# A decoder's first expert layer on one core: the down product of each expert as three rounded passes

## The chip, the cores and the metric

One core of one Trainium2 chip. The time is device microseconds (us) of one execution of the kernel, the median of several runs. A profiled execution comes with it; its records give the start and length of each instruction on the five engines: TensorE (PE, with its weight loads as PEld), VectorE (DVE), ScalarE (ACT), GpSimd (POOL) and SyncE (SP), which here only issues DMA transfers.

## What is computed

Two decoder layers over 4 sequences of 256 tokens with 256 features, each of self-attention, a second mixing block and a mixture of experts, with layer norms between. The change lies in the first layer's mixture of experts. There are 32 experts, each token goes to 4 of them, and each expert has room for 256 tokens. Cut to that part:

```python
buf = jnp.zeros((E, C, x.shape[1]), x.dtype).at[sorted_eid, pos].set(x[tok], mode='drop')
gu = jnp.einsum('ech,ehf->ecf', buf, w13)
g, u = jnp.split(gu, 2, axis=-1)
act = jax.nn.silu(g) * u
eo = jnp.einsum('eci,eih->ech', act, w2)
```

with E = 32, C = 256, h = 256 and i = 128. All of it is float32.

## The kernel before

The kernel is one program of stages, each with its own buffers and semaphores; within a stage each engine runs its own list of instructions in order, and they wait for each other on semaphores. The stage of the change is `layer0_experts`. The stage before it scatters the tokens' rows into `k.slots` in DRAM, 256 slots an expert, and the stage after it gathers the results from `k.out_slots`.

The experts go one after the other. Four make a round (`RING` = 4), and the rounds are a hardware loop with the first and the last (for VectorE the first two) written out. Weights and rows lie in rings of four buffers, most intermediate tiles in rings of two. For expert e:

- SP (`load`, `load_down`, `store`, L928 to L945) loads the rows (256 KB), w13 (256 KB) and w2 (128 KB), and stores the result (256 KB). In its round it issues, per expert e: rows and w13 of e + 4, w2 of e + 3, and the store of e - 2. The load of w2 waits until the down product of e - 1 is done, the store until the result of e - 2 has been copied out. Before the rounds it issues rows and w13 of experts 0 to 3, and then w2 of experts 0 to 2.
- TensorE: `turn` (L995) transposes the rows in four 128x128 pieces into PSUM. `up` multiplies with w13 in rounded passes, through the helper `product` (L76 to L78). `down` (L1015) multiplies the activations with w2 in two plain float32 matmuls, which the profile records as four. The order in the round is turn(e + 1), up(e), down(e - 1).
- ScalarE: `keep_rows` (L1037) copies the turned rows from PSUM as rounded values, `cut_high` (L1042) rounds w13 of e + 2, and L1056 takes the silu of the gate half. In that order.
- GpSimd: `cut_low` (L974) subtracts the rounded w13 from w13.
- VectorE: `rows_low` (L1069) subtracts the rounded rows from the turned ones, L1080 multiplies silu and up half into `actT`, `keep_out` (L1064) copies the down product to SBUF. In that order, for e + 1, e and e - 1.

A rounded product splits each operand x into a rounded part x.h (type fp32r) and a rest x.l = x - x.h, and adds three passes:

```python
pe.matmul(out, left[0], right[1], start=start, stop=False)
pe.matmul(out, left[0], right[0], start=False, stop=False)
return pe.matmul(out, left[1], right[0], start=False, stop=stop)
```

`Parts` holds the pair of tiles. ScalarE also issues one transfer of the next layer's weights (1 MB, `layer1_prefetch`) after its first round.

Of the kernel before, what the change touches and what calls it, by code (L numbers as in the profile page):

```python
# [8 lines left out]
P = 128  # L9
# [887 lines left out]
def layer0_experts(nc, k, I):  # L897

    RING = 4
    with ExitStack() as stack:  # L900
# [5 lines left out]
        rowsT = Parts(m, "e_rowsT", [P, 2, DC * CAP])  # L906
        silu = m.sb("e_silu", [P, 2, CAP])
        actT = m.sb("e_actT", [P, 2, CAP])
        out = m.sb("e_out", [P, RING, 2, D])
        turn_ps = m.ps("e_turn_ps", [P, 2, 512])  # L910
        up_ps = m.ps("e_up_ps", [P, 2, 512])
# [2 lines left out]
        w_in = [m.sem(f"e_w_in{r}") for r in range(RING)]  # L914
        w2_in = [m.sem(f"e_w2_in{r}") for r in range(RING)]
        w_high, w_low = m.sem("e_w_high"), m.sem("e_w_low")
        stored = k.stored
        turned = m.sem("e_turned")
        rowsT_high, rowsT_low = m.sem("e_rowsT_high"), m.sem("e_rowsT_low")
# [6 lines left out]
        with nc.Block() as block:  # L926
            @block.sync
            def _(sp):  # L928
                def load(e, r):
                    at_least(sp, turned, e - RING + 1)  # L930
                    sp.dma_start(rows[:, r], k.slots[bass.ds(e * CAP, CAP), :].rearrange("(s p) d -> p s d", p=P)
                                 ).then_inc(rows_in[r], 16)
                    at_least(sp, w_low, e - RING + 1)
                    sp.dma_start(w13[:, r], I["L0_ffn_w13"][bass.ds(e, 1)].rearrange("a (c p) f -> p (a c) f", p=P)
                                 ).then_inc(w_in[r], 16)

                def load_down(e, r):
                    at_least(sp, down_done, e - RING + 1)
                    sp.dma_start(w2[:, r], I["L0_ffn_w2"][bass.ds(e, 1)].rearrange("a p d -> p (a d)")
                                 ).then_inc(w2_in[r], 16)  # L940

                def store(e, r):
                    sp.wait_ge(out_kept, e + 1)
                    sp.dma_start(k.out_slots[bass.ds(e * CAP, CAP), :].rearrange("(s p) d -> p s d", p=P), out[:, r]
                                 ).then_inc(stored[r], 16)  # L945

                def emit(rnd, first, last):
                    for r in range(RING):
                        e = RING * rnd + r
                        if not last:  # L950
                            load(e + RING, r)
                        if not last or r == 0:
                            load_down(e + RING - 1, (r - 1) % RING)
                        if not first or r >= 2:
                            store(e - 2, (r - 2) % RING)
                sp.wait_ge(k.scattered, NT * TOP0 * 16)
                for e in range(RING):
                    load(e, e)
                for e in range(RING - 1):
                    load_down(e, e)  # L960
                emit(0, True, False)
                with sp.Fori(1, E0 // RING - 1) as rnd:
                    emit(rnd, False, False)
                emit(E0 // RING - 1, False, True)
                for r in range(RING - 2, RING):
                    store(E0 - RING + r, r)
                for r in range(RING):
                    sp.wait_ge(stored[r], 16 * (E0 // RING))

            @block.gpsimd  # L970
            def _(pool):
                def cut_low(e, r):
                    pool.wait_ge(w_high, e + 1)
                    pool.tensor_tensor(w13_p.l[:, r], w13[:, r], w13_p.h[:, r], ALU.subtract).then_inc(w_low, 1)  # L974
                with pool.Fori(0, E0 // RING) as rnd:
                    for r in range(RING):
                        cut_low(RING * rnd + r, r)
# [10 lines left out]
            @block.tensor  # L988
            def _(pe):
                def turn(e, r, rnd):  # L990
                    pe.wait_ge(rows_in[r], 16 * (rnd + 1))
                    at_least(pe, rowsT_low, e - 1)
                    for c in range(DC):
                        for s in range(2):
                            last = pe.transpose(turn_ps[:, r % 2, c * CAP + s * P:c * CAP + (s + 1) * P],  # L995
                                                rows[:, r, s, c * P:(c + 1) * P], k.ident[:, :])
                    last.then_inc(turned, 1)

                def up(e, r, rnd):
                    pe.wait_ge(w_low, e + 1)  # L1000
                    pe.wait_ge(rowsT_low, e + 1)
                    at_least(pe, act_done, e - 1)
                    for j in range(2):
                        for c in range(DC):
                            last = product(pe, up_ps[:, r % 2, j * CAP:(j + 1) * CAP],
                                           w13_p[:, r, c, j * I0:(j + 1) * I0],
                                           rowsT[:, r % 2, c * CAP:(c + 1) * CAP], c == 0, c == DC - 1)
                    last.then_inc(up_done, 1)

                def down(e, r, rnd):  # L1010
                    pe.wait_ge(w2_in[r], 16 * (rnd + 1))
                    pe.wait_ge(act_done, e + 1)
                    at_least(pe, out_kept, e - 1)
                    for s in range(2):
                        last = pe.matmul(down_ps[:, r % 2, s * D:(s + 1) * D], actT[:, r % 2, s * P:(s + 1) * P],  # L1015
                                         w2[:, r, :], start=True, stop=True)
                    last.then_inc(down_done, 1)

                turn(0, 0, 0)

                def emit(rnd, first, last):
                    for r in range(RING):
                        e = RING * rnd + r
                        if not (last and r == RING - 1):
                            turn(e + 1, (r + 1) % RING, rnd + (r == RING - 1))
                        up(e, r, rnd)
                        if not (first and r == 0):
                            down(e - 1, (r - 1) % RING, rnd - (r == 0))
                rounds(pe, emit)
                down(E0 - 1, RING - 1, E0 // RING - 1)  # L1030

            @block.scalar
            def _(act):
# [5 lines left out]
                def cut_high(e, r, rnd):  # L1039
                    act.wait_ge(w_in[r], 16 * (rnd + 1))  # L1040
                    at_least(act, up_done, e - RING + 1)
                    act.activation(w13_p.h[:, r], w13[:, r], ACT.Copy).then_inc(w_high, 1)  # L1042
                cut_high(0, 0, 0)
                keep_rows(0, 0)
                cut_high(1, 1, 0)

                def emit(rnd, first, last):
                    for r in range(RING):
                        e = RING * rnd + r
                        if not (last and r == RING - 1):  # L1050
                            keep_rows(e + 1, (r + 1) % RING)
                        if not (last and r >= RING - 2):
                            cut_high(e + 2, (r + 2) % RING, rnd + (r >= RING - 2))
                        act.wait_ge(up_done, e + 1)
                        at_least(act, act_done, e - 1)
                        act.activation(silu[:, r % 2, :], up_ps[:, r % 2, 0:CAP], ACT.Silu).then_inc(silu_done, 1)  # L1056
                rounds(act, emit, beside=layer1_prefetch)

            @block.vector
            def _(dve):  # L1060
# [6 lines left out]
                def rows_low(e, r):  # L1067
                    dve.wait_ge(rowsT_high, e + 1)
                    dve.tensor_tensor(rowsT.l[:, r % 2, :], turn_ps[:, r % 2, :], rowsT.h[:, r % 2, :], ALU.subtract  # L1069
                                      ).then_inc(rowsT_low, 1)  # L1070
                rows_low(0, 0)

                def emit(rnd, first, last):
                    for r in range(RING):
                        e = RING * rnd + r
                        if not (last and r == RING - 1):
                            rows_low(e + 1, (r + 1) % RING)
                        dve.wait_ge(silu_done, e + 1)
                        at_least(dve, down_done, e - 1)
                        dve.tensor_tensor(actT[:, r % 2, :], silu[:, r % 2, :], up_ps[:, r % 2, CAP:2 * CAP], ALU.mult  # L1080
                                          ).then_inc(act_done, 1)
                        if not (first and r == 0):
                            keep_out(e - 1, (r - 1) % RING, rnd - (r == 0))
                rounds(dve, emit, peeled=2)
                keep_out(E0 - 1, RING - 1, E0 // RING - 1)

# [1982 lines left out]
```

## Time and profile before

| | us |
|---|---|
| median of 3 runs | 1152.67 (1152.44 to 1154.89) |
| the profiled execution | 1150.72 |
| its span | 1148.8 |
| TensorE busy in the span | 1027.6 (89%) |
| VectorE, ScalarE, GpSimd busy | 722.9, 570.5, 473.5 |
| mean granted TensorE clock | 0.951 of full |

The experts' stage lies between about 392 and 489 us of the span. The span is what the trace covers; the profiled execution's own time is 1.9 longer, for what lies around it. Busy shares are means over stages that have different limits, so the stage is read by itself, in its windows and its timeline. Timeline rows give start, length, engine, line, and the tiles written and read; several instructions of a kind in a row are merged (x4), and what ended the engine's idle time stands in brackets.

### The profile page before, as it was taken

The page shows a single profiled execution, that of the slowest core. Times are in us where ns is not written, and L with a number is a line of the kernel's source. Part 1 is how long each engine was busy: PE and PEld are TensorE (multiplying, and loading weights), DVE is VectorE, ACT ScalarE, POOL GpSimd, SP SyncE. Part 2 cuts the span into 40 slices and gives each one's busy share as a digit, 9 for nine tenths or more (in the row PEclk, how much of TensorE's full clock was granted, in tenths as well). Part 3 has the DMA queues.
Part 4 walks back from the last instruction along what each step waited for, and adds up shares of the span by engine and source line. Part 5 has one row for each costly group of instructions (what it writes and reads, how often), then busy time and mean ns, then how long its engine had stood idle before and what let it go on. Part 6 is the DMA issues. An engine that isn't in the chain of part 4 may idle for free. (4 is left out here: it accounts for less than half of the span.)

```text
span 1148.8 us, 19245 instructions
## 1 busy us (share of the span) xinstructions
PE 1027.6 (89%) x6044; PEld 830.0 (72%) x6044; DVE 722.9 (63%) x2000; ACT 570.5 (50%) x1568; POOL 473.5 (41%) x507
## 2 busy tenths in 40 slices
PE   4999999999994599939899999988987889999995
PEld 3888888887883399917778888856444568787785
DVE  5878777776365356636665663115687648788775
ACT  2355445545222155426676773026775545655553
POOL 5776777673257544366211110010035313444322
PEclk9999999999997699969999999988998989999998
DMA  9600000000001499832401101001003011112101
GB/s 314 265 28 28 27 14 27 27 14 1 1 28 57 130 322 333 284 110 83 152 24 60 29 19 38 1 21 49 2 2 111 1 55 55 56 56 66 45 1 38
DMA packets 83481, 85.41 MB, mean 74 GB/s; under 512 B 8545, under 2 KB 75943, under 8 KB 83280
## 3 DMA queue, kind: packets, MB, share of 16 engines
q1 hardware_dynamic: 76944, 67.00, 18.3%
q10 hardware_dynamic: 3392, 10.16, 2.3%
q0 software_dynamic: 3072, 7.34, 2.1%
q8 instruction: 38, 0.62, 0.2%
q14 instruction: 35, 0.29, 0.1%
HBM read 63.36 MB, written 22.02 MB: 74 GB/s over the span
## 5 line engine op out<-in xcount | busy, mean ns | idle before, releaser
L514 POOL TENSOR_TENSOR a_qk<-h,a_by_sin 128x512 f32<-128x512 f32 x64 | 89.1, 1392 | 5.0
L294 ACT ACTIVATE a_probsT<-a_turn_ps 128x384 f32<-128x384 f32 x128 | 61.7, 482 | 43.4 <-PE a_turn_ps L253 43.4
L322 DVE CUSTOM_DVE_ANT_0 h<-a_score_ps,mask_bf 128x128 f32<-128x128 f32 (+1 forms) x128 | 40.8, 356 | 60.6 <-PE a_score_ps L315 60.0
L76 PE MATMUL a_proj_ps<-a_x_l,a_w_h 128*128 128x512 f32 x128 | 57.5, 449 | 16.9 <-POOL a_w_l L519 16.5
L1235 POOL TENSOR_TENSOR a_w_l<-a_w,a_w_h 128x256 fp32r<-128x256 f32 x30 | 21.9, 730 | 111.6 <-ACT a_w_h L1428 111.5
L278 ACT ACTIVATE y_moe<-a_score_ps,a_nmax 128x128 f32<-128x128 f32 x64 | 23.5, 368 | 87.5 <-DVE a_nmax L271 87.5
L411 PEld LDWEIGHTS a_proj_ps<-a_w,xT 128*128 128x128 f32 x512 | 62.6, 193 | 2.7 <-issue 0.5
L411 PE MATMUL a_proj_ps<-a_w,xT 128*128 128x128 f32 x512 | 62.8, 276 | 0.1
L974 POOL TENSOR_TENSOR e_w_l<-e_w,e_w_h 128x512 fp32r<-128x512 f32 x32 | 40.9, 1278 | 52.8 <-ACT e_w_h L1042 52.8
L699 PE MATMUL t_y_ps<-wo,attnT 128*128 128x256 f32 x256 | 57.2, 380 | 0.0
L2483 POOL TENSOR_TENSOR m_up_l<-m_up_w,m_up_h 128x1024 fp32r<-128x1024 f32 x8 | 19.4, 2426 | 90.0 <-ACT m_up_h L2455 90.0
L1475 PE MATMUL p_y_ps<-wo,attnT 128*128 128x256 f32 x256 | 55.5, 379 | 0.8 <-PEq L1207 0.8
L1475 PEld LDWEIGHTS p_y_ps<-wo,attnT 128*128 128x128 f32 x256 | 48.6, 190 | 7.5 <-issue 0.9
L287 DVE TENSOR_SCALAR y_moe<-y_moe,a_rtotal 128x128 f32<-128x128 f32 x64 | 52.3, 818 | 2.3
L699 PEld LDWEIGHTS t_y_ps<-wo,attnT 128*128 128x128 f32 x256 | 47.9, 190 | 6.1
L78 PE MATMUL a_proj_ps<-a_x_h,a_w_l 128*128 128x512 f32 x128 | 51.9, 405 | 0.0
L77 PE MATMUL a_proj_ps<-a_x_h,a_w_h 128*128 128x512 f32 x128 | 51.7, 404 | 0.0
L463 DVE TENSOR_TENSOR h<-a_proj_ps,cos_q 128x512 f32<-128x512 f32 x32 | 22.1, 692 | 44.7 <-PE a_proj_ps L78 44.7
L328 ACT ACTIVATE h<-h,a_nmax 128x128 f32<-128x128 f32 x64 | 25.7, 402 | 46.9 <-DVE a_nmax L322 44.2
L467 DVE STREAM_SHUFFLE hT<-a_proj_ps 128x512 f32<-128x512 f32 x64 | 47.1, 736 | 0.0
L510 POOL TENSOR_TENSOR a_by_sin<-hT,sin_q 128x512 f32<-128x512 f32 x32 | 40.9, 1279 | 14.1 <-DVE hT L467 14.1
L510 POOL TENSOR_TENSOR a_by_sin<-hT,sin_k 128x512 f32<-128x512 f32 x32 | 41.3, 1291 | 9.6 <-DVE hT L467 9.6
(436 smaller groups left out, 3383.2 us busy)
## 6 DMA issues: line engine op xcount, KB each, us to landing
slots<-zeros ACTq DMA_DIRECT2D x4, 2048.0 KB, 16.1
e_rows<-slots SPq DMA_DIRECT2D x32, 256.0 KB, 4.7
e_w<-in_L_ffn_w_dram SPq DMA_DIRECT2D x32, 256.0 KB, 4.8
out_slots<-e_out SPq DMA_DIRECT2D x32, 256.0 KB, 4.3
e_w<-in_L_ffn_w_dram SPq DMA_DIRECT2D x32, 128.0 KB, 4.3
a_w<-in_L_attn_w_q_dram SPq DMA_DIRECT2D x32, 128.0 KB
m_up_w<-in_up_dram SPq DMA_DIRECT2D x8, 512.0 KB, 4.0
a_w<-in_L_attn_Wq_dram SPq DMA_DIRECT2D x16, 128.0 KB, 2.2
```

What stands on the lines that cost most here:

```text
L76: pe.matmul(out, left[0], right[1], start=start, stop=False)
L77: pe.matmul(out, left[0], right[0], start=False, stop=False)
L78: return pe.matmul(out, left[1], right[0], start=False, stop=stop)
L287: dve.tensor_scalar(self.probs[:, b, 0:P], self.probs[:, b, 0:P], self.rtotal[:, b, 0:1], None, ALU.mult)
L294: act.activation(self.probsT[:, b % 2, :], self.turn_ps[:, b % 2, 0:CAUSAL], ACT.Copy).then_inc(self.turned_kept, 1)
L411: last = pe.matmul(proj_ps[:, c % 2, t * HD:(t + 1) * HD], k.xT[:, kc, half * HALF + t * P:half * HALF + (t + 1) * P], w[:, par, 2, kc, :] ...
L467: dve.stream_shuffle(swapped[:, r, :], proj_ps[:, c % 2, :], [i ^ 1 for i in range(32)]).then_inc(rot_in, 1)
L510: pool.tensor_tensor(by_sin[:, r2, :].rearrange("p (b s) -> p b s", b=2), swapped[:, r, :].rearrange("p (b s) -> p b s", b=2), sin[:, None ...
L514: pool.tensor_tensor(qk[:, par, 0 if what == "q" else 1, half * HALF:(half + 1) * HALF], by_cos[:, r, :], by_sin[:, r2, :], ALU.add).then_ ...
L699: last = pe.matmul(y_ps[:, t % 2, 0:D], k.ctxT[:, h, t * P:(t + 1) * P], k.wo[:, h, :], start=h == 0, stop=h == H - 1)
L974: pool.tensor_tensor(w13_p.l[:, r], w13[:, r], w13_p.h[:, r], ALU.subtract).then_inc(w_low, 1)
L1475: last = pe.matmul(y_ps[:, t % 2, 0:D], k.ctxT[:, h, t * P:(t + 1) * P], k.wo[:, h, :], start=h == 0, stop=h == H - 1)
```

## The change

The down product of this stage takes the same three rounded passes as the up product. w2 is split by ScalarE (`cut_high`) and GpSimd (`cut_low`), each right behind its work on w13, and the activations by ScalarE (`keep_act`) and VectorE (`act_rest`), one expert later than they are made: in round position e, ScalarE's keep_act(e - 1) stands behind keep_rows(e + 1), and VectorE's act_rest(e - 1) behind rows_low(e + 1). The down product waits for both rests (w2_low, act_low) where it waited for w2's transfer and for actT. The load of w2 waits for w2_low in place of the down product. New tiles: `e_w2_h`, `e_w2_l` (rings of four) and `e_actT_h`, `e_actT_l` (rings of two).

```diff
@@ -906,6 +906,7 @@
         rowsT = Parts(m, "e_rowsT", [P, 2, DC * CAP])
         silu = m.sb("e_silu", [P, 2, CAP])
         actT = m.sb("e_actT", [P, 2, CAP])
+        w2_p, actT_p = Parts(m, "e_w2", [P, RING, D]), Parts(m, "e_actT", [P, 2, CAP])
         out = m.sb("e_out", [P, RING, 2, D])
         turn_ps = m.ps("e_turn_ps", [P, 2, 512])
         up_ps = m.ps("e_up_ps", [P, 2, 512])
@@ -914,6 +915,8 @@
         w_in = [m.sem(f"e_w_in{r}") for r in range(RING)]
         w2_in = [m.sem(f"e_w2_in{r}") for r in range(RING)]
         w_high, w_low = m.sem("e_w_high"), m.sem("e_w_low")
+        w2_high, w2_low = m.sem("e_w2_high"), m.sem("e_w2_low")
+        act_high, act_low = m.sem("e_act_high"), m.sem("e_act_low")
         stored = k.stored
         turned = m.sem("e_turned")
         rowsT_high, rowsT_low = m.sem("e_rowsT_high"), m.sem("e_rowsT_low")
@@ -935,7 +938,7 @@
                                  ).then_inc(w_in[r], 16)
 
                 def load_down(e, r):
-                    at_least(sp, down_done, e - RING + 1)
+                    at_least(sp, w2_low, e - RING + 1)
                     sp.dma_start(w2[:, r], I["L0_ffn_w2"][bass.ds(e, 1)].rearrange("a p d -> p (a d)")
                                  ).then_inc(w2_in[r], 16)
 
@@ -972,6 +975,8 @@
                 def cut_low(e, r):
                     pool.wait_ge(w_high, e + 1)
                     pool.tensor_tensor(w13_p.l[:, r], w13[:, r], w13_p.h[:, r], ALU.subtract).then_inc(w_low, 1)
+                    pool.wait_ge(w2_high, e + 1)
+                    pool.tensor_tensor(w2_p.l[:, r], w2[:, r], w2_p.h[:, r], ALU.subtract).then_inc(w2_low, 1)
                 with pool.Fori(0, E0 // RING) as rnd:
                     for r in range(RING):
                         cut_low(RING * rnd + r, r)
@@ -1008,12 +1013,12 @@
                     last.then_inc(up_done, 1)
 
                 def down(e, r, rnd):
-                    pe.wait_ge(w2_in[r], 16 * (rnd + 1))
-                    pe.wait_ge(act_done, e + 1)
+                    pe.wait_ge(w2_low, e + 1)
+                    pe.wait_ge(act_low, e + 1)
                     at_least(pe, out_kept, e - 1)
                     for s in range(2):
-                        last = pe.matmul(down_ps[:, r % 2, s * D:(s + 1) * D], actT[:, r % 2, s * P:(s + 1) * P],
-                                         w2[:, r, :], start=True, stop=True)
+                        last = product(pe, down_ps[:, r % 2, s * D:(s + 1) * D],
+                                       actT_p[:, r % 2, s * P:(s + 1) * P], w2_p[:, r, :])
                     last.then_inc(down_done, 1)
 
                 turn(0, 0, 0)
@@ -1040,6 +1045,14 @@
                     act.wait_ge(w_in[r], 16 * (rnd + 1))
                     at_least(act, up_done, e - RING + 1)
                     act.activation(w13_p.h[:, r], w13[:, r], ACT.Copy).then_inc(w_high, 1)
+                    act.wait_ge(w2_in[r], 16 * (rnd + 1))
+                    at_least(act, down_done, e - RING + 1)
+                    act.activation(w2_p.h[:, r], w2[:, r], ACT.Copy).then_inc(w2_high, 1)
+
+                def keep_act(e, r):
+                    act.wait_ge(act_done, e + 1)
+                    at_least(act, down_done, e - 1)
+                    act.activation(actT_p.h[:, r % 2, :], actT[:, r % 2, :], ACT.Copy).then_inc(act_high, 1)
                 cut_high(0, 0, 0)
                 keep_rows(0, 0)
                 cut_high(1, 1, 0)
@@ -1049,12 +1062,15 @@
                         e = RING * rnd + r
                         if not (last and r == RING - 1):
                             keep_rows(e + 1, (r + 1) % RING)
+                        if not (first and r == 0):
+                            keep_act(e - 1, (r - 1) % RING)
                         if not (last and r >= RING - 2):
                             cut_high(e + 2, (r + 2) % RING, rnd + (r >= RING - 2))
                         act.wait_ge(up_done, e + 1)
                         at_least(act, act_done, e - 1)
                         act.activation(silu[:, r % 2, :], up_ps[:, r % 2, 0:CAP], ACT.Silu).then_inc(silu_done, 1)
                 rounds(act, emit, beside=layer1_prefetch)
+                keep_act(E0 - 1, RING - 1)
 
             @block.vector
             def _(dve):
@@ -1068,6 +1084,11 @@
                     dve.wait_ge(rowsT_high, e + 1)
                     dve.tensor_tensor(rowsT.l[:, r % 2, :], turn_ps[:, r % 2, :], rowsT.h[:, r % 2, :], ALU.subtract
                                       ).then_inc(rowsT_low, 1)
+
+                def act_rest(e, r):
+                    dve.wait_ge(act_high, e + 1)
+                    dve.tensor_tensor(actT_p.l[:, r % 2, :], actT[:, r % 2, :], actT_p.h[:, r % 2, :], ALU.subtract
+                                      ).then_inc(act_low, 1)
                 rows_low(0, 0)
 
                 def emit(rnd, first, last):
@@ -1075,13 +1096,16 @@
                         e = RING * rnd + r
                         if not (last and r == RING - 1):
                             rows_low(e + 1, (r + 1) % RING)
+                        if not (first and r == 0):
+                            act_rest(e - 1, (r - 1) % RING)
                         dve.wait_ge(silu_done, e + 1)
-                        at_least(dve, down_done, e - 1)
+                        at_least(dve, act_low, e - 1)
                         dve.tensor_tensor(actT[:, r % 2, :], silu[:, r % 2, :], up_ps[:, r % 2, CAP:2 * CAP], ALU.mult
                                           ).then_inc(act_done, 1)
                         if not (first and r == 0):
                             keep_out(e - 1, (r - 1) % RING, rnd - (r == 0))
                 rounds(dve, emit, peeled=2)
+                act_rest(E0 - 1, RING - 1)
                 keep_out(E0 - 1, RING - 1, E0 // RING - 1)
 
 
```

## Rows read from the trace of the kernel before

**Rows 1.** Windows of 5 us: busy time of each engine (instructions), granted clock, DMA share, GB/s.

```profile
415.00:420.00 5.00, 4.23 (x33) 3.86 (x32) 1.92 (x4) 2.63 (x6) 1.81 (x2) 1.00 1.08 377
425.00:430.00 5.00, 5.00 (x39) 4.68 (x38) 3.54 (x8) 2.97 (x6) 2.77 (x3) 1.00 1.09 376
```

**Rows 2.** Timeline of all engines over one expert: start, length, engine, line, tiles.

```profile
479.09 0.60 PE L995 MATMUL e_turn_ps<-ident,e_rows 128*128 128x128 f32 x4
...
479.65 0.28 PE L77 MATMUL e_up_ps<-e_rowsT_h,e_w_h 128*128 128x256 f32 x1
...
479.73 0.60 ACT L1037 ACTIVATE e_rowsT_h<-e_turn_ps 128x512 fp32r<-128x512 f32 x1 [0.87 <-PE e_turn_ps L995]
...
480.36 0.69 DVE L1069 TENSOR_TENSOR e_rowsT_l<-e_turn_ps,e_rowsT_h 128x512 fp32r<-128x512 f32 x1 [0.38 <-ACT e_rowsT_h L1037]
...
480.37 0.63 ACT L1042 ACTIVATE e_w_h<-e_w 128x512 fp32r<-128x512 f32 x1
...
480.97 1.03 PE L1015 MATMUL e_down_ps<-e_w,e_actT 128*128 128x256 f32 x4
481.08 1.27 POOL L974 TENSOR_TENSOR e_w_l<-e_w,e_w_h 128x512 fp32r<-128x512 f32 x1 [1.14 <-ACT e_w_h L1042]
481.17 0.38 ACT L1056 ACTIVATE e_silu<-e_up_ps 128x256 f32<-128x256 f32 x1 [0.16 <-PE e_up_ps L78]
...
481.83 0.49 PE L995 MATMUL e_turn_ps<-ident,e_rows 128*128 128x128 f32 x3
```

**Rows 3.** Groups by line and shape, 388 to 560: the nearest splits of 128x256 tiles.

```profile
L1358 DVE TENSOR_TENSOR c_p_l<-xT,c_p_h 128x256 fp32r<-128x256 f32 x5 | 2.1, 418 | 1.5 <-ACT c_p_h L1404 1.3 <-issue 0.2
...
L1428 ACT ACTIVATE a_w_h<-a_w 128x256 fp32r<-128x256 f32 x8 | 3.3, 409 | 4.5 <-DMA a_w<-in_L_attn_w_q_dram 4.4
...
L1235 POOL TENSOR_TENSOR a_w_l<-a_w,a_w_h 128x256 fp32r<-128x256 f32 x6 | 4.4, 734 | 12.8 <-ACT a_w_h L1428 12.7
```

**Rows 4.** Timeline of VectorE: two instructions with nothing to wait for between them.

```profile
417.69 0.68 DVE L1064 COPY e_out<-e_down_ps 128x512 f32<-128x512 f32 x1
418.29 0.68 DVE L1069 TENSOR_TENSOR e_rowsT_l<-e_turn_ps,e_rowsT_h 128x512 fp32r<-128x512 f32 x1
```

**Rows 5.** Timeline: the stage's last expert, and rounded passes that start from a stop.

```profile
486.62 0.42 DVE L1080 TENSOR_TENSOR e_actT<-e_silu,e_up_ps 128x256 f32<-128x256 f32 x1 [1.16 <-ACT e_silu L1056]
...
487.11 0.73 PEld L1015 LDWEIGHTS e_down_ps<-e_w,e_actT 128*128 128x128 f32 x4 [0.48 <-issue]
488.28 0.69 DVE L1064 COPY e_out<-e_down_ps 128x512 f32<-128x512 f32 x1 [0.52 <-PE e_down_ps L1015]
...
515.07 0.19 PEld L76 LDWEIGHTS a_job_ps<-c_p_l,a_w_h 128*128 128x128 f32 x1
...
515.41 0.19 PEld L78 LDWEIGHTS a_job_ps<-c_p_h,a_w_l 128*128 128x128 f32 x1
```

**Rows 6.** Timeline: the start of the stage.

```profile
395.73 1.56 SPq L939 DMA_DIRECT2D e_w<-in_L_ffn_w_dram  x3
...
397.93 0.56 PE L76 MATMUL e_up_ps<-e_rowsT_l,e_w_h 128*128 128x256 f32 x1
...
404.10 0.60 PE L995 MATMUL e_turn_ps<-ident,e_rows 128*128 128x128 f32 x4
```

**Rows 7.** The page's DMA issues: count, KB each, median us from issue to landing.

```profile
e_w<-in_L_ffn_w_dram SPq DMA_DIRECT2D x32, 256.0 KB, 4.8
...
e_w<-in_L_ffn_w_dram SPq DMA_DIRECT2D x32, 128.0 KB, 4.3
...
a_w<-in_L_attn_Wq_dram SPq DMA_DIRECT2D x16, 128.0 KB, 2.2
```

**Rows 8.** Timeline of VectorE and GpSimd in the next layer's attention.

```profile
542.94 1.88 DVE L1342 SCALAR_TENSOR_TENSOR y_moe<-attnT,weight,y_moe 128x256 f32<-128x256 f32 x3
543.28 0.75 POOL L1235 TENSOR_TENSOR a_w_l<-a_w,a_w_h 128x256 fp32r<-128x256 f32 x1 [0.95 <-ACT a_w_h L1428]
...
555.63 1.52 DVE L1342 SCALAR_TENSOR_TENSOR y_moe<-attnT,weight,y_moe 128x256 f32<-128x256 f32 x3
```

## The prediction

> **What bounds the kernel now.** I read the views in the order of the rows. The windows come first: in the experts' stage TensorE is busy all the time at the full granted clock (1.00, 2.4 GHz), while in 5 us VectorE is busy 3.5, ScalarE 3.0 and GpSimd 2.8 [rows 1]. The DMA engines are full as well (share 1.09, 376 GB/s), but TensorE waits for none of it there, so its own work sets the pace. The timeline of one expert shows what that work is [rows 2]. Call the start of the four transposes S (479.09). They last until S+0.36, the twelve passes of the up product until S+1.88 (480.97), the down product until S+2.74 (481.83), where the next expert begins. From the second pass (479.65) to the down product (480.97) eleven passes take 1.32, so a rounded pass follows the one before it after 0.12; the down product, two plain matmuls recorded as four passes, takes 0.86 (480.97 to 481.83).
>
> The same rows give the rhythm of the others. ScalarE rounds the next expert's turned rows from S+0.64 (479.73), VectorE makes their rest from S+1.27 (480.36), ScalarE's silu comes at S+2.08 and VectorE's product with it right after. All of it is early: the rest of the rows is done at S+2.0 and wanted after the next transposes (S+3.1), the activations are wanted by the down product at S+4.6.
>
> **The change, part by part.**
>
> Down product on TensorE: four records (0.86) become six rounded passes at 0.12, 0.72. By itself that would give 0.14 an expert, 2.60 instead of 2.74.
>
> New work on the others, per expert. ScalarE: two roundings of 128x256, 0.41 each [rows 3], on some 1.6 of 2.74 (3.0 of 5 us [rows 1]): 2.4. VectorE: one subtraction of 128x256, 0.42, on some 1.9: 2.3. GpSimd: one of 0.73 on 1.27 [rows 2, 3]: 2.0. No engine comes above 2.60 in sum, though ScalarE comes near. In throughput the change would pay.
>
> The order is what I think decides. In expert e TensorE issues turn(e+1), up(e), down(e-1), and down now waits for act_low of e-1. VectorE makes that rest behind rows_low(e+1), in the same queue, and rows_low(e+1) waits for ScalarE's rounding of the rows that turn(e+1) has just produced. So the down product of e-1 hangs on the transposes of e+1, issued in the same round. Step by step from S:
> - ScalarE's keep_rows(e+1) starts at S+0.64, rows_low(e+1) at S+1.27 [rows 2].
> - keep_act(e-1) follows on ScalarE after at most 0.64, as the weights' rounding does now (479.73 to 480.37 [rows 2]): from S+1.28 to S+1.7, in time.
> - VectorE starts its next instruction 0.60 after a 128x512 one when that one's wait is met [rows 4]: act_rest(e-1) runs from S+1.87 to S+2.29. TensorE wanted it at S+1.88.
> - VectorE's end to the weight load that waits for it is 0.07 (487.04 to 487.11) [rows 5].
> - Rounded passes that start from a stop have their third load, with which the second matmul starts, 0.34 after the first load (515.07 to 515.41) [rows 5]; flowing passes take 0.24. Then five more steps of 0.12 to the next transposes: 0.94, so 1.01 after act_rest's end.
>
> The sum is a period of 2.29 + 1.01 = 3.30 us. Least: no restart cost, 2.29 + 0.07 + 0.72 = 3.08. Most: act_rest only behind rows_low's full 0.69 (S+1.96 to 2.38) and 0.10 more where passes give way to transposes: 3.49. I take 3.30, as both pieces come from rows of the same form.
>
> The stage goes from the transposes at 404.10 [rows 6] to those at 481.83, 28 experts in 77.73, and one more at 2.74: 80.5 for 29. At 3.30 they take 95.7: **+15.2** (8.8 to 20.7). A wait at 415 that the 77.73 contains (busy 4.23 of 5 us [rows 1]) goes away in this.
>
> Start of the stage. ScalarE's first instruction was the rounding of w13 of expert 0; now that of w2 of expert 0 follows before keep_rows(0), and it waits for a transfer that SP issues only behind all four experts' rows and w13, at 395.73 [rows 6]. 128 KB transfers of this stage land 4.3 after issue in the median [rows 7]: at 400.0. With the rounding, keep_rows(0) starts at about 400.3, its rest ends at 401.7, and up(0), at 397.93 now [rows 6], starts then: **+3.8**. Least: landing 2.2 after issue, as 128 KB did in the quiet first stage, 1.8; most: 4.8 as the 256 KB ones, 4.3. I take 4.3, since the queues are full with the rows and w13 issued ahead.
>
> SP's queue: load_down no longer waits for a down product but for w2_low, some three experts old, so SP issues every load about one expert earlier; next it waits at the store for keep_out. Transfers get more time and ScalarE's new wait for w2 (needed two experts ahead, not at the down product) has, by my count, 6 us from issue. I cost it at nothing; the cover is the longer period. If it went, silu could slip 0.8 before the chain feels it.
>
> End of the stage. Now silu, product, down product and keep_out (488.28) follow each other [rows 5]. keep_act (0.41) and act_rest (0.42) come between; act_rest also stands some 0.2 behind keep_out(30), the hand-overs take 0.07, and the passes give 0.14 back: **+0.95** (0.6 without the queueing and the hand-overs, 1.2 with all of them doubled).
>
> GpSimd's two subtractions, 2.0 from S+2.2 or 2.4 on, end by S+1.1 of the next round, before the next are due: nothing. keep_out and silu shift inside gaps: nothing.
>
> **Sum:** 3.8 + 15.2 + 0.95 = 20.0. The profiled execution took 1150.72 (span 1148.8); it becomes 1170.7. The median of the runs, 1152.67, is 1.95 above it, and I add the same 20.0: 1172.7.
>
> **A rule of the skill against this change.** Around 543 VectorE runs three accumulations, each with two inputs in SBUF, beside a GpSimd subtraction: 1.88, against 1.52 for the same three alone [rows 8]. So the two engines do block each other in such forms. act_rest is the first VectorE instruction in this stage with both inputs in SBUF. The Trainium skill (SBUF — State Buffer, Who interferes with whom) says that such an instruction and a GpSimd one that reads SBUF exclude each other for a whole instruction; by that rule, the trace agrees. By the positions above, GpSimd starts 0.71 after ScalarE's rounding of w13 (480.37 to 481.08 [rows 2]), which now stands behind keep_act: at S+2.2 to 2.4, after act_rest has begun; its last one ended by S+1.1. GpSimd would lose 0.1, act_rest nothing.
>
> **Rivals.**
> 1. The two engines collide after all, by the mechanism of [rows 8]: if GpSimd slips so far that it is still subtracting at S+1.87 (a slip of 0.8), or act_rest comes 0.3 to 0.5 late, act_rest waits for a running subtraction of 1.27. Half of it on average, 0.64 x 29 = 18.6 more: 1191. Against it: both orders follow from the same instruction on ScalarE. 8%.
> 2. Not slower: the parts are ready in time and TensorE stays the bound. This needs act_rest done by S+1.88, and w2(0) in by about 396. Then 31 x 0.14 = 4.3 are gained, 1148.3; with the start's 3.8 and the end's 0.95 it comes out at 1153. Against it: the rows' rest alone ends at S+1.96 now, and VectorE runs in order. 5%, of which 2% for faster, 2 to 3% for the same.
> 3. The clock falls, since TensorE stands still some 0.6 of 3.3 us. Against it: from 415 to 420 it was busy 4.23 of 5 us, about as much, and kept 1.00 [rows 1]. At half clock TensorE's own 2.60 become 5.2, longer than the chain: 29 x 1.9 = 55 more, 1228. 3%.
> 4. The chain is there but only the start or only part of it counts (VectorE's order less binding than I read it): some 8 to 12 more than now, 1161 to 1165. 7%, inside the range.
>
> The forecast's own case has 77%. About 0.2% (2.3 us) is what a measurement of this kernel can tell from no change. **Chances:** faster 0.02, same 0.03, slower 0.95.
>
> **Range.** The terms' ends add to 11.2 (1.8, 8.8, 0.6) and 26.2 (4.3, 20.7, 1.2): 1164 to 1179. I widen it to 1161 for case 4 and to 1186 for part of case 1; what is left out is some 15%.
>
> **What would show it.** Right: in the middle of the stage transposes 3.3 apart; TensorE idle 0.4 to 0.6 before each down product, released by VectorE's act_rest; act_rest starting 0.6 behind rows_low; first up product near 401.7; DMA share below 1, and ScalarE's waits for w13 gone. Wrong: a period of 2.6 to 2.75 (case 2), act_rest longer than 0.42 with GpSimd busy (case 1), clock below 1 in the stage (case 3), ScalarE waiting for w2 in every expert.

## The result, and the profile after

| | before | after |
|---|---|---|
| median, us | 1152.58 | 1171.64 (1166.87 to 1175.38) |
| ratio | | 1.0164 [1.0136, 1.0192] |
| profiled execution, its span | 1150.72, 1148.8 | 1166.87, 1165.0 |
| first transposes to the last keep_out | 394.38 to 488.28: 93.90 | 393.94 to 506.80: 112.86 |
| the rest of the span behind that | 660.5 | 658.2 |

The change costs 19.1 us; 1172.7 was forecast. The profiled execution of after is its fastest, 4.8 below its median. Its experts' stage is 18.96 longer than before, as much as the medians differ by, and what comes behind the stage happened to be 2.3 shorter. That rest lay between 654.9 and 664.4 in all the traces below, with code that none of them changes, so each kernel is read by its ratio and by the length of the stage, not by the span of one trace.

The windows of after, in the columns of [rows 1]:

```profile
405.00:410.00 5.00, 5.00 (x33) 5.00 (x32) 2.47 (x5) 2.97 (x7) 2.76 (x4) 0.70 0.59 178
415.00:420.00 5.00, 4.50 (x38) 4.30 (x38) 3.12 (x7) 2.72 (x7) 3.25 (x4) 1.00 0.87 297
425.00:430.00 5.00, 4.63 (x40) 4.46 (x39) 3.40 (x7) 3.02 (x8) 3.11 (x4) 1.00 1.04 340
440.00:445.00 5.00, 4.13 (x34) 3.89 (x33) 3.02 (x8) 2.69 (x8) 3.63 (x4) 1.00 0.89 255
```

From 440 to 445 no engine is full and the DMA share is 0.89: a chain of waits sets the pace. The granted clock is 1.00 (2.4 GHz) in every window from 410 to the end of the stage; it was lower only behind the late start, 0.70 from 405 to 410. The timeline of after shows the chain; where [rows 2] had S = 479.09, S is 441.23 here:

```profile
441.23 0.60 PE L1000 MATMUL e_turn_ps<-ident,e_rows 128*128 128x128 f32 x4
...
441.86 0.60 ACT L1042 ACTIVATE e_rowsT_h<-e_turn_ps 128x512 fp32r<-128x512 f32 x1 [1.18 <-PE e_turn_ps L1000]
...
442.36 0.41 ACT L1055 ACTIVATE e_actT_h<-e_actT 128x256 fp32r<-128x256 f32 x1
...
442.49 0.69 DVE L1085 TENSOR_TENSOR e_rowsT_l<-e_turn_ps,e_rowsT_h 128x512 fp32r<-128x512 f32 x1 [0.38 <-ACT e_rowsT_h L1042]
...
443.10 0.42 DVE L1090 TENSOR_TENSOR e_actT_l<-e_actT,e_actT_h 128x256 fp32r<-128x256 f32 x1
443.19 0.40 ACT L1050 ACTIVATE e_w_h<-e_w 128x256 fp32r<-128x256 f32 x1
443.36 1.30 POOL L977 TENSOR_TENSOR e_w_l<-e_w,e_w_h 128x512 fp32r<-128x512 f32 x1 [1.19 <-ACT e_w_h L1047]
...
443.76 0.38 PE L76 MATMUL e_down_ps<-e_w_l,e_actT_h 128*128 128x256 f32 x1 [0.50 <-DVE e_actT_l L1090]
```

Keep_rows at S+0.63, keep_act at S+1.13, rows_low at S+1.26, act_rest at S+1.87, and TensorE idle for 0.50, released by act_rest's tile. GpSimd's w13 subtraction begins 0.26 after act_rest. This expert has the longer of two steps, 3.34; in the usual one TensorE stands 0.37 (at 450.15). The restart of a usual step, one expert earlier, in three rows of that timeline (act_rest, the down product's first and third weight load):

```profile
439.92 0.41 DVE L1090 TENSOR_TENSOR e_actT_l<-e_actT,e_actT_h 128x256 fp32r<-128x256 f32 x1
...
440.41 0.19 PEld L76 LDWEIGHTS e_down_ps<-e_w_l,e_actT_h 128*128 128x128 f32 x1 [0.54 <-issue]
...
440.63 0.19 PEld L78 LDWEIGHTS e_down_ps<-e_w_h,e_actT_l 128*128 128x128 f32 x1
```

The first load comes 0.08 after act_rest's end, the third load 0.22 after the first, and the next transposes (441.23) 0.82 after the first. The period is 1.87 + 0.41 + 0.08 + 0.82 = 3.18, and 3.34 once in each pass of the four-expert loop.

The start of the stage, against [rows 6], and its end, against [rows 5]:

```profile
393.94 1.12 PE L1000 MATMUL e_turn_ps<-ident,e_rows 128*128 128x128 f32 x4 [7.11 <-DMA e_rows<-slots]
...
395.27 1.48 SPq L942 DMA_DIRECT2D e_w<-in_L_ffn_w_dram  x3
...
400.40 0.42 ACT L1050 ACTIVATE e_w_h<-e_w 128x256 fp32r<-128x256 f32 x1 [5.07 <-DMA e_w<-in_L_ffn_w_dram]
400.72 0.58 ACT L1042 ACTIVATE e_rowsT_h<-e_turn_ps 128x512 fp32r<-128x512 f32 x1
...
402.17 0.55 PE L76 MATMUL e_up_ps<-e_rowsT_l,e_w_h 128*128 128x256 f32 x1 [4.78 <-DVE e_rowsT_l L1085]
...
504.36 0.42 DVE L1103 TENSOR_TENSOR e_actT<-e_silu,e_up_ps 128x256 f32<-128x256 f32 x1 [0.83 <-ACT e_silu L1071]
...
504.81 0.42 ACT L1055 ACTIVATE e_actT_h<-e_actT 128x256 fp32r<-128x256 f32 x1 [0.49 <-DVE e_actT L1103]
505.29 0.42 DVE L1090 TENSOR_TENSOR e_actT_l<-e_actT,e_actT_h 128x256 fp32r<-128x256 f32 x1
505.78 0.19 PEld L76 LDWEIGHTS e_down_ps<-e_w_l,e_actT_h 128*128 128x128 f32 x1 [1.37 <-issue]
...
506.80 0.69 DVE L1080 COPY e_out<-e_down_ps 128x512 f32<-128x512 f32 x1 [1.08 <-PE e_down_ps L78]
```

keep_rows(0) is ready at once and stands behind w2(0), which ScalarE waits 5.07 us for. ScalarE's waits for w2 in the whole stage are 6.1 us in three: this one, 0.89 and 0.15.

### The profile page after: what moved, and what is told of

The parts are those of the page before. It is cut to its first block and busy times, and to the rows that moved or that the text cites. A ratio compares the mean times of both kernels' runs of the same rounds, so it can differ in the third digit from the quotient of the medians.

```text
span 1165.0 us, 19553 instructions
## 1 busy us (share of the span) xinstructions
PE 1027.4 (88%) x6108; PEld 830.6 (71%) x6108; DVE 736.3 (63%) x2032; ACT 586.9 (50%) x1632; POOL 495.9 (43%) x539
## 5 line engine op out<-in xcount | busy, mean ns | idle before, releaser
L1259 POOL TENSOR_TENSOR a_w_l<-a_w,a_w_h 128x256 fp32r<-128x256 f32 x30 | 21.8, 728 | 112.0 <-ACT a_w_h L1452 111.8
L519 POOL TENSOR_TENSOR a_w_l<-a_w,a_w_h 128x256 fp32r<-128x256 f32 x32 | 23.5, 755 | 51.9 <-ACT a_w_h L546 51.9
```

## The experiments

My theory: two positions in two queues (rows_low ahead of act_rest on VectorE, keep_rows ahead of keep_act on ScalarE) tie the down product to the transposes of the same round; w2(0) costs the start. Rivals: the passes themselves, the added work on ScalarE and GpSimd, a collision of VectorE and GpSimd. All times in one table; "stage" is the first transposes to the last keep_out in the trace (93.90 before), "to 4th" from the first to the fourth transposes (9.72 before), "step" the usual distance of transposes in the middle (2.74 before).

| kernel | median | ratio, interval | stage | to 4th | step |
|---|---|---|---|---|---|
| after | 1171.64 | 1.0164 [1.0136, 1.0192] | 112.86 | 14.95 | 3.18 |
| e13_again | 1172.51 | 1.0168 [1.0135, 1.0201] | 113.31 | 15.61 | 3.18 |
| e1_act_order | 1203.08 | 1.0430 [1.0384, 1.0476] | 144.70 | 16.58 | 4.26 |
| e2_dve_order | 1167.88 | 1.0116 [1.0078, 1.0153] | 108.02 | 14.82 | 2.89 |
| e3_both_orders | 1164.72 | 1.0093 [1.0064, 1.0122] | 104.71 | 14.76 | 2.59 to 2.98 |
| e7_plain_same_waits | 1176.36 | 1.0208 [1.0165, 1.0252] | 117.77 | 15.39 | 3.33 |
| e6_weights_only | 1172.31 | 1.0156 [1.0121, 1.0190] | 110.94 | 14.63 | 2.74 to 3.99 |
| e8_weights_early_load | 1161.52 | 1.0066 [1.0045, 1.0087] | 102.45 | 15.10 | 2.74 |
| e5_start | 1172.11 | 1.0160 [1.0124, 1.0196] | 110.16 | 9.72 | 3.18 |
| e11_late_w2 | 1173.44 | 1.0170 [1.0142, 1.0198] | 110.15 | 12.31 | 3.18 |
| e9_orders_late_w2 | 1151.41 | 0.9988 [0.9962, 1.0015] | 94.06 | 12.47 | 2.59 |
| e10_orders_late_start | 1150.03 | 0.9977 [0.9958, 0.9996] | 90.75 | 9.42 | 2.59 |
| e12_late_prefetch | 1151.63 | 0.9989 [0.9969, 1.0008] | 91.85 | 10.80 | 2.59 |

### The changed kernel once more

> The changed kernel unchanged, for its spread beside the three others on one chip: 1169 to 1174, median near 1171.6, ratio 1.016; a median outside 1168 to 1175 would say that differences of 3 us between these kernels need more runs than were made.

As expected: 1172.51. Medians of these kernels are uncertain by some 2 us, so 3 us between two of them is little.

### VectorE's order alone

```
                     for r in range(RING):
-                        if not (last and r == RING - 1):
-                            rows_low(e + 1, (r + 1) % RING)
                         if not (first and r == 0):
                             act_rest(e - 1, (r - 1) % RING)
+                        if not (last and r == RING - 1):
+                            rows_low(e + 1, (r + 1) % RING)
```

> Only VectorE's order is turned: act_rest(e-1) ahead of rows_low(e+1). Chain theory: act_rest now hangs on ScalarE's keep_act, which ends at S+1.54 after the transposes' start S, so act_rest runs S+1.57 to S+1.99; with 0.30 to the second pass and 0.60 to the next transposes the period is 2.89 instead of 3.18, 29 x 0.29 = 8 us less than the changed kernel, about 1163. Rival, the sum of the added work is what slows the stage: the same work in another order, still 3.18 and 1171.6.

The step fell to 2.89, the figure expected: the order on VectorE is a link of the chain, worth 0.29. The time fell less, because one step grew to 6.38 (421.21 to 427.59), behind a wait of ScalarE for w2:

```profile
423.99 0.42 ACT L1050 ACTIVATE e_w_h<-e_w 128x256 fp32r<-128x256 f32 x1 [3.61 <-DMA e_w<-in_L_ffn_w_dram]
```

### ScalarE's order alone

The same exchange on ScalarE: keep_act(e-1) ahead of keep_rows(e+1).

> Only ScalarE's order is turned: keep_act(e-1) ahead of keep_rows(e+1). Chain theory (the down product waits for VectorE's act_rest, which stands behind rows_low): nothing moves, transposes stay 3.18 us apart (3.34 once in four experts), time as the changed kernel, 1171.6 within 2. Rival, the rounding on ScalarE comes too late: with keep_act 0.8 us earlier the period falls to 2.6 to 2.9 and the time to about 1155 to 1163.

A miss, by 31 us. The timeline of this kernel (S = 438.21):

```profile
439.34 0.62 ACT L1047 ACTIVATE e_w_h<-e_w 128x512 fp32r<-128x512 f32 x1
439.48 0.69 DVE L1085 TENSOR_TENSOR e_rowsT_l<-e_turn_ps,e_rowsT_h 128x512 fp32r<-128x512 f32 x1 [0.38 <-ACT e_rowsT_h L1042]
...
440.05 1.26 POOL L977 TENSOR_TENSOR e_w_l<-e_w,e_w_h 128x512 fp32r<-128x512 f32 x1 [2.12 <-ACT e_w_h L1047]
440.09 1.50 DVE L1090 TENSOR_TENSOR e_actT_l<-e_actT,e_actT_h 128x256 fp32r<-128x256 f32 x1
```

The rounding of w13 now comes at S+1.13, as keep_act has moved away from between it and keep_rows, so GpSimd starts at S+1.84 and not S+2.13, 0.04 before act_rest. Act_rest takes 1.50 instead of 0.42, in all 20 of its records from 410 to 495 (mean 1500 ns), and the step grows by the same 1.08: 3.18 to 4.26. This is rival 1's mechanism, set off not by a slip of GpSimd but by its coming 0.3 earlier. The Trainium skill (SBUF — State Buffer, Who interferes with whom) says that an instruction of VectorE with two inputs in SBUF contends with a GpSimd one that reads SBUF, under an exclusive lock, and that the order of issue decides who blocks. By that rule, the trace agrees, all but 0.14: act_rest lasts 1.22 from 440.09 to GpSimd's end and 0.28 more, where its 0.42 alone would make 1.64. It goes the other way too: GpSimd's next subtraction, of w2, begins at 441.27 while act_rest still runs, and takes 0.91 on average instead of 0.73.

### Both orders

> Both orders turned: the activations are split before the new rows. Chain theory: act_rest is over by S+1.35, TensorE never stops, period 2.60, 28 x (3.22 - 2.60) = 17 less, about 1154, with the start still 4.2 later than in the kernel before. Rival of the added work: 3.18, 1171.6. Rival of the two engines' shared reads: act_rest, at S+0.95, meets GpSimd's subtraction of w2 (to S+1.3 or so) and takes over 0.42; if it meets more than that, it ends after S+1.88 and the period is above 2.60.

The step reached 2.58 to 2.60, but not throughout. Beside e2's 2.89 that is what ScalarE's order is worth, 0.30; only this pair shows it, as the same exchange alone (e1) ran into the collision. ScalarE in the timeline of this kernel (the prefetch is layer 1's 1024 KB of w_kv):

```profile
416.17 0.47 ACTq L1162 DMA_DIRECT2D hT<-in_L_attn_w_kv_dram  x1
...
420.43 0.62 ACT L1047 ACTIVATE e_w_h<-e_w 128x512 fp32r<-128x512 f32 x1
...
426.04 0.42 ACT L1050 ACTIVATE e_w_h<-e_w 128x256 fp32r<-128x256 f32 x1 [4.98 <-DMA e_w<-in_L_ffn_w_dram]
426.36 0.36 ACT L1071 ACTIVATE e_silu<-e_up_ps 128x256 f32<-128x256 f32 x1
```

w2 for two experts ahead is late, and silu, which belongs to the present expert and was ready, is queued behind it: 5 us of stop for weights that nobody wants yet. ScalarE waited for w2 in nine places, 14.0 us in all, of which 5.6 at the start. TensorE's clock was 0.68 in the window 425 to 430, where TensorE was busy 1.79 of 5 us, and 0.64 in the next, full one. This is the wait that the prediction costed at nothing: in the changed kernel it is 1 us in all after the start, with steps of 3.18; once the steps are 2.6 the cover is gone.

### The passes alone, and the parts of the weights alone

e7 keeps every instruction and wait of the change but stores the high parts unrounded, as float32, and makes the down product from them in two plain matmuls:

```
-                        last = product(pe, down_ps[:, r % 2, s * D:(s + 1) * D],
-                                       actT_p[:, r % 2, s * P:(s + 1) * P], w2_p[:, r, :])
+                        last = pe.matmul(down_ps[:, r % 2, s * D:(s + 1) * D], actT_p.h[:, r % 2, s * P:(s + 1) * P],
+                                         w2_p.h[:, r, :], start=True, stop=True)
```

> All waits, orders and instructions of the changed kernel except the down product itself: the rounded tiles are float32 copies and the product is two plain matmuls, so nothing is rounded there. If six rounded passes are worth 0.14 us an expert less than the plain product also behind a stop, the period is 3.3 instead of 3.18 and the time 3 to 5 us above the changed kernel, about 1175. If the passes' restart eats the gain, the period stays 3.18.

The step is 3.33, 0.15 more than 3.18: what the six passes save (0.14 by the prediction). The waits, with the work that they put in order, cost 0.59 an expert (3.33 less 2.74).

e6 makes w2's parts but not those of the activations; the down product is the plain one and, reading w2 itself, keeps SyncE's old gate on the next load:

```
                 def load_down(e, r):
                     at_least(sp, w2_low, e - RING + 1)
+                    at_least(sp, down_done, e - RING + 1)
...
-                    pe.wait_ge(act_low, e + 1)
+                    pe.wait_ge(act_done, e + 1)
```

> Only w2's parts are made (ScalarE and GpSimd) and waited for; the activations are not split and the down product is the plain one of the kernel before. Chain theory: period 2.74, as before, and only the later start remains, 4.2 less the stall at 415 (0.9) that may vanish: 1152.6 + 3.3 to 4.2, about 1156. Rival of the added work: ScalarE's 0.41 more already lengthens the period above 2.74, over 1158.

A miss. ScalarE's line in the table of waits (total, times, longest) of this kernel from 400 to 515:

```profile
ACT e_w_h L1051 <- DMA e_w<-in_L_ffn_w_dram: 46.6, 28, 5.4
```

The load is released as late as before the change, but ScalarE wants it some two experts earlier. The moved gate of load_down is thus no side matter: the change needs it.

e8 is e6 with that gate as in the change (the down product reads ScalarE's copy of w2, kept in float32).

> As the run with the weights' parts alone, but SP's load of w2 keeps the changed kernel's early gate (w2_low); the plain down product reads a float32 copy of w2. Theory formed on the last runs: the 17 us of that run came from ScalarE waiting 28 times for a w2 still on its way, because the load was gated by the down product while ScalarE wanted it two experts ahead. Then here ScalarE does not wait, period 2.74, only the later start is left: about 1156 to 1158. Rival, ScalarE's added rounding is what slows it: again above 1165.

The step is 2.74, that of before: the rounding and the subtraction of w2 cost no step, in throughput they are hidden. What they cost is once only: 5.4 from the first to the fourth transposes (15.10 against 9.72), and steps of 5.14 and 4.09 behind the prefetch. The stage is 8.55 longer, 1.0066 in the ratio. That puts the time between theory and rival. ScalarE still waits for w2 here, 26.6 us in 22 places from 400 to 515; behind the start and the prefetch these waits, 1.81 at most, fall into its slack, but for one step of 3.18.

### The start

SyncE issues w2(0) to w2(2) each right behind its expert's w13, in the changed kernel:

```
                 for e in range(RING):
                     load(e, e)
-                for e in range(RING - 1):
-                    load_down(e, e)
+                    if e < RING - 1:
+                        load_down(e, e)
```

> The changed kernel with SP issuing w2 of experts 0, 1 and 2 right behind their rows and w13. Start theory (keep_rows(0) waits behind the rounding of w2(0), issued too late): w2(0) is issued about 3 us earlier and lands about 397.5 instead of 400.4, so the first up product starts near 399.5 instead of 402.2; period unchanged 3.18; 2.5 to 3 us less than the changed kernel. Rival, the start is bound by bandwidth: nothing is gained, since the bytes ahead only change places.

The start came back in full (first up product at 398.50; 9.72 to the fourth transposes, as before), but the median did not move: steps of 5.35 and 3.73 now stand at 417.47, behind the prefetch issued at 409.85. Not all of it is ScalarE's wait for w2 (1.45 and 0.36): in the first of these steps GpSimd started 0.06 ahead of act_rest, and the collision of e1 came with it, the only one in this kernel from 410 to 495:

```profile
419.99 1.26 POOL L977 TENSOR_TENSOR e_w_l<-e_w,e_w_h 128x512 fp32r<-128x512 f32 x1 [0.95 <-ACT e_w_h L1047]
420.05 1.48 DVE L1090 TENSOR_TENSOR e_actT_l<-e_actT,e_actT_h 128x256 fp32r<-128x256 f32 x1
```

The stage keeps 2.7 of the 5.2 gained, less than these medians resolve. The expectation's rival, that bandwidth binds the start, is out.

e11 leaves SyncE alone and makes w2's parts one expert later, ScalarE w2(e+1) behind w13(e+2), GpSimd w13(e+1) and then w2(e).

> The changed kernel with one edit: w2's parts are made one expert later (ScalarE rounds w2(e+1) right behind w13(e+2), GpSimd takes w13(e+1) and then w2(e)); orders of keep_rows, keep_act and the two subtractions as in the change. My theory: the period stays at 3.18 in three of four experts, for it is the chain from the transposes through keep_rows, keep_act, rows_low and act_rest; the start gets back 2 to 4 us (first up product by 399 instead of 402.17), 1168 to 1169. Rival: as with SyncE's order changed alone, the gain is lost again in a stall near 421 and the time stays at 1171 to 1172. A period under 3.1 would say that GpSimd's or ScalarE's work on w2 was part of it.

The step stayed 3.18, as it must if the chain sets it; of the start 2.6 came back (12.31 to the fourth), and the ratio is that of e13 beside it. The rival was right on the time but not on its reason: no step near 421 is longer than 3.35. The stage is 2.7 shorter than in the changed kernel, and the medians don't show it.

### All causes removed together

e9: both orders, and w2 one expert later as in e11.

> Both orders turned and w2 split one expert later (ScalarE rounds w2 of e+1 behind w13 of e+2; at the start behind keep_rows(0)). Theory: what kept the run with both orders above 1154 was ScalarE's wait for w2, 5 us once beside the 1 MB prefetch and 0.3 to 1 us often, with silu queued behind it; one expert more of time for the transfer ends it. Period 2.60, first up product within 1 us of the kernel before: 1149 to 1151. Rival, bandwidth: the transfers of an expert (896 KB) cannot come every 2.60 us, TensorE waits for rows or w13 instead and the time stays near 1155 to 1160.

1151.41, even with before. The step is 2.59 without the scatter of e3, so bandwidth does not bind it, against the rival. One longer step is left behind the prefetch, 4.24. e10 adds SyncE's order of e5.

> The kernel of the third order experiment (both keep-order edits and w2's split one expert later, 1151.41) with SyncE issuing w2(0..2) right behind the rows and w13 of the same expert. My theory: that kernel's start stall (transpose at 401.19, the next only at 408.03, 6.84 instead of 2.58) is ScalarE's rounding of w2(0) waiting for a load issued ninth in the queue; issued third, it lands before it is wanted, the transposes stand at about 401.2, 403.9, 406.6, and the time falls by 3 to 4 us, to 1148. The rival, which the start experiment on the changed kernel speaks for: what the start gains is lost again where layer 1's 1 MB prefetch is issued (the stall of 4.24 at 421.21 grows to 6 or 7), and the time stays at 1150 to 1152.

1150.03, ratio 0.9977 [0.9958, 0.9996]: the fastest version, and barely faster than before. My theory was right on the start (9.42 to the fourth transposes), the step behind the prefetch didn't grow (4.04), and the stage is 3.3 shorter than e9's; but the medians show only 1.4 of that, so the time itself lies where the rival had put it. Its timeline, and its windows in the columns of [rows 1]:

```profile
442.51 0.42 ACT L1067 ACTIVATE e_actT_h<-e_actT 128x256 fp32r<-128x256 f32 x1 [0.56 <-DVE e_actT L1118]
442.59 0.74 POOL L981 TENSOR_TENSOR e_w_l<-e_w,e_w_h 128x256 fp32r<-128x256 f32 x1
...
442.83 0.58 ACT L1052 ACTIVATE e_rowsT_h<-e_turn_ps 128x512 fp32r<-128x512 f32 x1
...
442.96 0.65 DVE L1105 TENSOR_TENSOR e_actT_l<-e_actT,e_actT_h 128x256 fp32r<-128x256 f32 x1
...
443.53 0.68 DVE L1100 TENSOR_TENSOR e_rowsT_l<-e_turn_ps,e_rowsT_h 128x512 fp32r<-128x512 f32 x1
```

```profile
412.00:417.00 5.00, 5.00 (x45) 5.00 (x44) 4.48 (x8) 3.01 (x7) 3.36 (x4) 1.00 0.95 350
417.00:422.00 5.00, 3.77 (x33) 3.60 (x32) 3.18 (x6) 3.53 (x9) 3.36 (x4) 1.00 1.09 378
...
450.00:455.00 5.00, 5.00 (x45) 5.00 (x43) 4.22 (x8) 4.13 (x10) 3.72 (x5) 1.00 1.08 379
```

TensorE is busy all of 450 to 455 again, with 2.59 an expert: the 2.60 of the prediction's throughput sum. Act_rest still collides, with GpSimd's w2 subtraction, and takes 0.67 on average, but it ends at 443.61, about when TensorE wants it.

### Layer 1's prefetch

e12 is e10 with that transfer issued by ScalarE behind the fourth round of four experts:

```
-                rounds(act, emit, beside=layer1_prefetch)
+                rounds(act, emit, peeled=4, beside=layer1_prefetch)
```

> The previous kernel with layer 1's 1 MB prefetch issued by ScalarE behind its fourth round of four experts instead of the first. My theory: the stall near 421 is this transfer taking bandwidth while the rings of weights are still short, so the step of 4 to 6 us there goes and a smaller one, at most 1 us longer than its neighbours, stands near 450, where the rings are full; another 1.5 to 2.5 us, to about 1146. Rival one: the stall moves with the prefetch and keeps its size (step of 4 us near 450, time as in the kernel beside it). Rival two: the prefetch isn't its cause, and a step of over 4 us stays near 421.

```profile
442.28 0.41 ACTq L1177 DMA_DIRECT2D hT<-in_L_attn_w_kv_dram  x1
...
450.61 0.63 ACT L1057 ACTIVATE e_w_h<-e_w 128x512 fp32r<-128x512 f32 x1 [1.37 <-DMA e_w<-in_L_ffn_w_dram]
```

Rival one was right. The steps near 421 are 2.58 to 2.60, and one of 3.89 stands at 450.57, 8.3 after the issue; in e10 one of 4.04 stood at 417.23, 8.3 after the issue at 408.94. The prefetch is the cause of the stop, and the stop goes where it goes. Why the rings don't cover it later either is argued, not shown: the stage takes most of the bandwidth throughout (379 GB/s from 450 to 455 in e10), so they are likely no fuller there. That it is the cause was tried on this kernel alone; for the long steps of e2, e3, e5 and e8 only their place speaks.
## Why the prediction was right, by its steps

- **Total.** +20.0 forecast, +19.1 measured, for the reason given. That they are so close is in part luck: of the terms below the period was 2.3 too high, the start 1.4 too low and the end 0.15 too high. The positions in the chain (rows_low at S+1.27, act_rest from S+1.87 to S+2.29, the load 0.07 behind it) came out within 0.02; keep_act stood at S+1.13 instead of S+1.28, in time as forecast. e2 moved one link and the step fell by the 0.29 that the timeline gives.
- **The period.** 3.30 was 0.12 too much. The failing piece is the restart: I took 0.34 from first to third load from the next layer, and it is 0.22 here. Against that I had not foreseen the 0.16 more once in four steps; the load comes 0.23 and not 0.08 after act_rest's end there. All in all 28 steps took 90.23 instead of 77.73, which with 0.44 for one more expert is +12.9, where +15.2 stood.
- **The passes' gain** of 0.14: e7 shows 0.15.
- **The start.** +3.8 was too little. w2(0) was rounded 5.1 after its issue, outside my 4.3 and my upper bound of 4.8, and the first up product came at 402.17 for 401.7. Measured from the first transposes, which came 0.44 earlier, that is 4.7 later than before. From the first to the fourth transposes it is 5.2 (5.9 in e13): one step behind the late start is still 4.02, where before it was 3.46, at a clock of 0.70 between 405 and 410, where before it was 1.00. I had counted only up to up(0).
- **The end.** +0.95 forecast; from the last transposes to keep_out 7.68 instead of 6.45, 0.44 of which is the last longer expert: +0.8.
- **ScalarE's wait for w2 at nothing.** Right for this kernel by its long steps, as the text said of the cover, but the "6 us from issue" says nothing of the prefetch: the long steps of e3, e5 and e8 there add 3 to 7 us, as soon as either the steps or the start are faster.
- **The collision (rival 1).** Its price was some half of what it came to in e1 (1.08 an expert, not 0.64, because the two start together each time), and its condition was too narrow: 0.3 us less on ScalarE's way to GpSimd is enough. In the change itself act_rest was 416 ns on average; the margin is 0.26. The 0.1 that GpSimd was to lose to act_rest came out as 0.03 (1.305 on average from 410 to 495, 1.279 before).
- **The clock (rival 3)** did not fall in the chain: 1.00 from 410 on, with TensorE busy 4.1 to 4.6 of 5 us.
- **Not slower (rival 2)** needs more than its two conditions: e9 and e10 had to change both orders, the lag of w2 and SyncE's order. It then gives 0.9977, where 1148.3 was the most the passes could bring.

What stays open: why a loop boundary costs 0.16 in the chain-bound kernels, and whether the prefetch cut into small pieces would take its stop away; neither was tried.

## What to carry to other kernels

When a product gets new producers, write down for each engine's queue what stands ahead of them and what that in turn waits for: the throughput sum (2.60) said faster and the queue order said 3.18. Before a fix is called one, see what its shorter period uncovers: the removed links here brought out others (a shared port, a rounding two experts ahead with silu behind it, a prefetch). A wait for data of a later round should stand behind the present round's work in an in-order queue.

## What the runs showed of the hardware that I had not expected

- VectorE's subtraction of two SBUF tiles took 1.50 when GpSimd's 128x512 subtraction had begun 0.04 before it (e1), and 0.42 when GpSimd began 0.26 after it (after). In four cases the engine that came second lost 0.13 or 0.14 less than the two overlapped: 1.08 of 1.22 and GpSimd 0.18 of 0.32 in e1, 0.23 of 0.37 in e10 (the rows shown), GpSimd 0.03 of 0.16 in the changed kernel.
- Rounded passes restart after a stop with 0.22 from the first to the third load here, 0.34 in [rows 5]; why they differ wasn't tried.
- Behind a single 1024 KB transfer on ScalarE's queue one step of TensorE grew by 1.3 (e12) to 5.2 us (e3, 7.77 less 2.59); it began 6 to 8 us after the issue (e3 5.7, e5 7.6, e9, e10 and e12 8.3). Where steps were 3.18 or more and the start was late (the changed kernel, e13, e1, e7, e11), none grew.
- With the same code behind the stage, the rest of the span was 654.9 us where the whole execution's mean granted clock was 0.956 (e7) and 664.4 where it was 0.946 (e5), more than most differences studied here. The mean clock doesn't order them all: e2 had 662.7 at 0.942.
